# First attention: the order in which the next batch's four quantised inputs are made (K, V, Q, QX before; K, Q, V, QX after)

## The reference: what is computed

```python
ln_out = _ln(hidden_states, ln_w, ln_b)
q  = _fp8_linear_pertensor(ln_out, wq,  wq_scale,  q_in_scale)
k  = _fp8_linear_pertensor(ln_out, wk,  wk_scale,  k_in_scale)
v  = _fp8_linear_pertensor(ln_out, wv,  wv_scale,  v_in_scale)
qx = _fp8_linear_pertensor(ln_out, wqx, wqx_scale, qx_in_scale)
```

## Time and profile before

| what | value |
|---|---|
| median of 3 runs | 3307.08 us (3305.06 to 3311.99) |
| the profiled execution, its own time | 3308.09 us |
| its span | 3305.9 us |
| mean granted TensorE clock | 0.946 of full |
| PE busy | 2887.7 us (87%) |
| DVE, ACT, POOL busy | 1797.5, 1695.5, 1740.7 us |

### The profile page before, as it was taken

The page is one execution under the profiler, slowest core; times in us unless marked ns, Lnnn a source line. Parts: engine busy times, 40 slices in busy tenths (PEclk is TensorE's granted clock), DMA queues, the critical chain, the costliest instruction groups (busy, mean ns, idle before and its releaser), DMA issues. The chain is left out here.

```text
span 3305.9 us, 57383 instructions
## 1 busy us (share of the span) xinstructions
PE 2887.7 (87%) x16324; PEld 1656.1 (50%) x16325; DVE 1797.5 (54%) x5172; ACT 1695.5 (51%) x4502; POOL 1740.7 (53%) x2429
## 2 busy tenths in 40 slices
PE   4699999999999969999999997699899999634996
PEld 2366666666666635555555543344444444322663
DVE  3366656656666555343433444588888887321331
ACT  5577777777777623223332333466666666311332
POOL 6467766776677435345544543655555655241222
PEclk9899999999999989999999998899999999757998
DMA  6601100010011055445544565355545555327444
GB/s 239 223 27 36 49 29 29 35 51 29 29 35 45 30 192 155 134 134 160 153 135 133 159 183 134 74 107 106 108 105 109 109 104 106 101 84 273 85 83 105
DMA packets 459854, 348.33 MB, mean 105 GB/s; under 512 B 295728, under 2 KB 366512, under 8 KB 459696
## 3 DMA queue, kind: packets, MB, share of 16 engines
q1 hardware_dynamic: 396896, 267.79, 29.0%
q0 software_dynamic: 16640, 38.05, 5.7%
q10 hardware_dynamic: 46224, 41.36, 4.2%
HBM read 194.88 MB, written 93.50 MB: 87 GB/s over the span
## 5 line engine op out<-in xcount | busy, mean ns | idle before, releaser
L437 PE MATMUL a_mm<-a_w_hi,a_xq_hi 128*128 128x512 f16 x768 | 301.9, 393 | 65.2 <-POOL a_xq_lo L885 61.5
L1646 POOL TENSOR_TENSOR e_st<-e_st,e_ws_tile 128x1024 f32<-128x1024 f32 x64 | 123.7, 1933 | 429.8 <-PE e_y L1402 418.9
L601 DVE BATCH_NORM_STATS2 a_st<-a_mm 128x6 f32<-128x128 f32 x768 | 170.7, 284 | 326.1 <-PE a_mm L438 231.6
L750 ACT ACTIVATE a_nrm<-a_mm,a_sc_t 128x128 f32<-128x128 f32 x768 | 290.4, 472 | 106.3 <-POOL a_sc_t L903 106.1
L438 PE MATMUL a_mm<-a_w_hi,a_xq_lo 128*128 128x512 f16 x768 | 303.2, 395 | 0.0
L1440 ACT ACTIVATE e_hh<-e_ha 128x512 f16<-128x512 f32 x128 | 76.3, 596 | 415.8 <-PE e_ha L1387 414.4
L1535 DVE SCALAR_TENSOR_TENSOR e_hl<-e_ha,e_hh 128x512 f16<-128x512 f32 x128 | 88.4, 691 | 352.3 <-ACT e_hh L1440 351.8
L902 POOL TENSOR_TENSOR a_sc_t<-a_sc_t,a_mhalf 128x4 f32<-128x4 f32 x192 | 202.5, 1055 | 138.3 <-DVE a_sc_t L608 138.0
L1811 PE MATMUL a_mm<-l_wh,a_src_hi 128*128 128x512 f16 x512 | 200.1, 391 | 76.0 <-DVE a_vl L1893 41.7
L1400 PE MATMUL e_y<-e_w2h,e_hh 128*128 128x512 f16 x640 | 242.6, 379 | 0.0
L1401 PE MATMUL e_y<-e_w2l,e_hh 128*128 128x512 f16 x640 | 242.6, 379 | 0.0
(11 more groups left out here) (350 smaller groups left out, 8294.6 us busy)
## 6 DMA issues: line engine op xcount, KB each, us to landing
e_st<-in_w SPq DMA_DIRECT2D x128, 512.0 KB, 4.3
disp<-a_empty SPq DMA_DIRECT2D x16, 781.5 KB, 4.1
e_st<-in_w1b SPq DMA_DIRECT2D x32, 352.0 KB, 3.1
e_xb<-disp ACTq DMA_DIRECT2D x41, 260.5 KB
disp<-a_empty SPq DMA_DIRECT2D x4, 2605.0 KB, 21.5
e_xb<-disp SPq DMA_DIRECT2D x40, 260.5 KB, 4.4
a_cx<-in_ctxT SPq DMA_DIRECT2D x32, 256.0 KB, 3.2
a_stage<-in_wprojT SPq DMA_DIRECT2D x16, 512.0 KB, 4.8
```

The costliest lines, as they stand in the source:

```text
L437: pe.matmul(out, xq_hi[:, n, c, :], w_hi[:, t, c, :], start=(c == 0), stop=False)
L750: ins = act.activation(nrm[:, n % 2, i * P:(i + 1) * P], src[:, i * P:(i + 1) * P], ACT.Identity, bias=sc_t[:, n % 2, 3, i:i + 1], scale=s ...
```

## The change

`SETS` becomes K, Q, V, QX: set number 1 is now Q's input and number 2 V's. `SCALE_OF` maps the number to the place in `wsc`, `bsc` and `isc`, whose order stays.

```diff
-SETS = ["K", "V", "Q", "QX"]
+SETS = ["K", "Q", "V", "QX"]
+SCALE_OF = [0, 2, 1, 3]
...
                         ins = act.activation(y0[:, n, c, :], xn[:, c * P:(c + 1) * P], ACT.Identity,
-                                             bias=bsc[:, n, c:c + 1], scale=wsc[:, n, c:c + 1])
+                                             bias=bsc[:, SCALE_OF[n], c:c + 1], scale=wsc[:, SCALE_OF[n], c:c + 1])
...
-                        ins = pool.tensor_scalar(y0[:, n, c, :], xn[:, c * P:(c + 1) * P], wsc[:, n, c:c + 1],
-                                                 bsc[:, n, c:c + 1], ALU.mult, ALU.add)
+                        ins = pool.tensor_scalar(y0[:, n, c, :], xn[:, c * P:(c + 1) * P], wsc[:, SCALE_OF[n], c:c + 1],
+                                                 bsc[:, SCALE_OF[n], c:c + 1], ALU.mult, ALU.add)
...
             def in_scale(n):
-                return isc[:, n, :].unsqueeze(2).to_broadcast([P, KT, P])
+                return isc[:, SCALE_OF[n], :].unsqueeze(2).to_broadcast([P, KT, P])
```

## The result

The changed kernel takes 3321.67 us (median of 7, 3318.05 to 3325.2) against 3307.91 for the kernel before in the same comparison: ratio 1.0037, 95% interval 1.0025 to 1.0048. The ratio is close to that of the means and makes it 12.2 us slower; the medians are 13.8 us apart.

The account below looks back on a forecast made before the run. PE was taken to bound the kernel, busy 87% of the span. Ten half-clock stretches at 1.7 us, 17.0, less 7.6 us paid before, gave +9.4 on the median 3307.08: 3316.5 us, range 3305 to 3323.

Parts of the forecast that it names:

- Q0 starts at once: PE, each batch: Q0 no longer waits for its quantised input, removing 2.6 to 2.7 us at this place.
- The pause moves to `r_transpose` and its release time is unchanged: PE at L516: ACT's L787 still ends at 678.45, so the stall moves there, 3.15 us in one piece.
- The rival of POOL slowed by earlier DVE work: DVE's stats of Q0 beside POOL delay L516 by 0.64 us per batch: +9 more, 3325.5 us; chance 0.05.
- the main case: The wait moves and half clock comes in 9 to 13 of 14 batches: +7.7 to +14.5 us; chance 0.5.
- V0's wait is hidden: PE: V0 waits for the third set, ready at 673.98, but begins about 679.4, hidden by 5 us of cover.
- POOL's changed waits cost nothing: POOL's L879 waits for Q3 in set 1 and for an earlier job in set 2: nothing lost.
- batches 0 and 1 give nothing: First two batches: Q0 starts earlier, but later waits for POOL or the input load give it back: 0.
- The price of a half-clock stretch: PE clock: each stretch costs 1.7 us gross after the change, against 1.08 us net in the kernel before.
- Their number, 10: Stalls bringing half clock, of 14: three quarters is 10.5, rounded to 10, midway between one half and all.
- the forecast of +9.4: Whole kernel: ten half-clock stretches, 17.0, less 7.6 us paid before, so slower by 9.4 us, to 3316.5 us.
- The rule of the Trainium skill: PE clock: long idle gaps between matmul bursts return the array to half rate, so one longer gap is worse than two shorter.
- Taken strictly, with all 14: Rival: every PE stall brings half clock, n = 14, +16.2 us, 3323.3 us; chance 0.12.

Follow-up runs that it names:

- experiments 1: Changed kernel with PE's r_transpose placed behind V0's projection and the scores of the same slot: 3267.83 us, ratio 0.9874 to the kernel before.
- 4: Changed kernel with ACT's copy of score group 4 ahead of the normalisation of job 0 in slot 1: 3264.59 us, ratio 0.9864.
- 8: Changed kernel with POOL's low part of the context input moved from slot 0 to slot 1: 3279.08 us, ratio 0.991.
- filled against filled: Extra matmuls put in PE's pause: changed kernel, 14 ahead of r_transpose's wait, 3304.81 us; kernel before, 12 ahead of Q0's wait, 3301.74 us.
- experiments 2: Kernel before with r_transpose placed behind V0's projection and the scores: 3301.93 us, ratio 0.9975.
- 6: Kernel before with ACT's copy of score group 4 ahead of the normalisation of job 0 in slot 1: 3301.52 us, ratio 0.9973.
- both repairs: Changed kernel with r_transpose behind V0 and the scores, and ACT's copy of score group 4 ahead of the normalisation: 3263.78 us, ratio 0.986.

## Why the prediction was right, point by point

- **Q0 starts at once.** Right: the two starts are 0.89 us apart, with no wait for L751.
- **The pause moves to `r_transpose` and its release time is unchanged.** Right, and shown from both sides: experiments 1 and 4 remove the pause by letting PE or ACT change its order, and 8 shortens it through POOL. Predicted 3.15 us, measured 3.34. The difference is POOL's scale factors for job 0, which come 0.17 later, L904 at 0.37 in place of 0.20.
- **The rival of POOL slowed by earlier DVE work** is that difference, at 0.2 us per batch and not 0.64. It came on top of the main case: 14 × 0.20 = 2.8 us, where filled against filled has 3 by the times and 2.5 in the traces. That a neighbour on DVE is the cause rests on the rows, slow beside L92 or L93 in every batch and in both kernels, and was not isolated by a run.
- **V0's wait is hidden, POOL's changed waits cost nothing, batches 0 and 1 give nothing.** Right, by the waits and the rows above, but for 0.4 us that the first two batches lost.
- **The price of a half-clock stretch: 1.7 us gross, 1.08 net before.** After: 67.90 − 66.22 = 1.68. Right. For the kernel before, 7 × 1.08 = 7.6 us was predicted and 8.9 measured by filling.
- **Their number, 10.** Measured 11, the first of them double, 0.9 us more. This term and the 2.8 us are what the forecast of +9.4 lacks: 11 × 1.69 + 0.9 − 7.6 + 2.8 = 14.7 us by rows. A part of it can be held against the traces: from the first to the last `r_transpose`, 13 batches, there are 10 of these stretches, the double one among them, and 6 before, so 10 × 1.69 + 0.9 − 6 × 1.08 + 13 × 0.20 = 13.9, and the traces have 14.3 ((1091.75 − 212.91) − (1077.77 − 213.24)). By the times, the clock is worth 17.9 − 8.9 = 9.0 us and the rest 3.3; that these add up to the 12.2 but for rounding follows from how they are taken and proves nothing.
- **That 10 came so near 11 is in part luck.** It was put midway between two rows by the length of the pause, and length alone does not fix the number: the same pause of 2.59 us brought half clock in 7, 6 and 4 of 14 batches in three kernels (before, experiments 2 and 6). What decides which pause is hit was not shown.
- **The rule of the Trainium skill** that long gaps bring the array to half rate (TensorE: Matmul & The Clock Gate, "Why this matters for your kernels") pointed the right way: 11 of 14 with the longer gap, 7 of 14 with the shorter. Taken strictly, with all 14, its +16.2 was only a little farther from the measured 12.2 than +9.4, but three gaps of 3.34 to 3.35 us kept full clock; here the measurement decides.

The main case happened, with one mechanism of a rival, at a third of its size, added to it.

The best kernel found has the change and both repairs, or ACT's alone: 3264 us, 1.4% under the kernel before.

## What to carry to other kernels

A short wait that is seen only in every second iteration, just behind a long one, is the next bound showing itself: before removing the long wait, work out when the second one would be released, and whether its release depends on the first. Here one edit alone cost 12 us, another alone saved 9, and together they saved 43. And a pause of the same length can cost more in another place, since a stretch at half clock in front of a wait is partly paid for (1.08 us net here), and one behind the last wait is not (1.68).

## What the runs showed of the hardware

- In batches 2 to 15, one trace for each kernel, pauses of 2.6 us, one in a batch, brought half clock in 7 batches of 14, and in 6 and 4 of 14 in two variants whose batch was 0.6 us shorter; pauses of 3.34 to 3.57 us brought it in 11 of 14, pauses of 1.5 us and less in none.
- Matmuls that do nothing useful made the kernel faster: 196 of them gained 17.9 us in the changed kernel, and 168 of them 8.9 us in the kernel before.
- The same 128x4 product on POOL took 0.37 to 0.40 us in 14 batches in which DVE's L92 or L93 ran beside it, and 0.20 us in the 14 batches of the kernel before, in which neither did.
